# Tables, projection and the first layer's edges in one block, K and V stored ahead of Q, rings of 8 and 16 gathered chunks, and one index load for 8 chunks

## The reference, cut to what matters

```python
# layer 0, 8 heads of 16 features
Q, K, V, Eh = x @ WQ, x @ WK, x @ WV, edge_attr @ WE
score = exp(clip((K[src] * Q[dst] / sqrt(16) * Eh).sum(per head), -5, 5))
h = x + segment_sum(V[src] * score, dst) / (segment_sum(score, dst) + 1e-6)
x = layernorm(x + batchnorm(h))
# layer 1, one head
xl = x @ W
e = leaky_relu((xl @ att_src)[src] + (xl @ att_dst)[dst], 0.2)
e = exp(e - segment_max(e, dst)[dst])
out = segment_sum(e / segment_sum(e, dst)[dst] * xl[src], dst) + bias
x = layernorm(x + (bn_relu(bn_relu(out @ W1 + b1) @ W2 + b2) + x))
```

## Time and profile before

| | |
|---|---|
| Median of three runs | 5932.58 us (5929.43 to 5944.88) |
| Profiled execution | 5944.3 us, span 5942.5 us |
| PE busy, PEld busy | 4076.5 us (69%), 3506.1 us (59%) |
| DVE busy | 3282.2 us (55%) |
| ACT busy | 1399.3 us (24%) |
| POOL busy | 3368.5 us (57%), of it 3272.3 us in the 3328 gathers |
| Granted TensorE clock, mean | 0.659 |
| DMA | 482,022 packets, 538.82 MB |

### The profile page before, as it was taken

One profiled execution on the slowest core, in us unless ns is written; L12 is line 12 of the kernel. 1 busy time (PEld: TensorE's weight loads), 2 busy tenths in 40 slices (PEclk: granted clock), 3 DMA queues, 4 the chain that ended last, 5 costly groups with the idle time before them and its releaser, 6 DMA issues. The chain is left out here.

```text
span 5942.5 us, 93441 instructions
## 1 busy us (share of the span) xinstructions
PE 4076.5 (69%) x21439; PEld 3506.1 (59%) x21440; DVE 3282.2 (55%) x8432; ACT 1399.3 (24%) x4197; POOL 3368.5 (57%) x3417
## 2 busy tenths in 40 slices
PE   5888888888888888888455555555555555555553
PEld 3777787887777777777423444444444444444431
DVE  5554555555555555555474555555555555555555
ACT  2111111111111111111043222222222222222224
POOL 1565555565556555656334666666666666666621
PEclk8787877777778777878676555555555555555566
DMA  7444444444444444444522222222222222222223
GB/s 215 119 126 121 125 123 122 124 125 124 123 123 128 121 123 124 127 121 130 99 58 70 50 51 49 51 50 50 50 51 50 50 51 49 50 51 50 51 69 85
DMA packets 482022, 538.82 MB, mean 91 GB/s; under 512 B 250299, under 2 KB 341053, under 8 KB 481366
## 3 DMA queue, kind: packets, MB, share of 16 engines
q0 software_dynamic: 133120, 330.78, 21.5%
q1 hardware_dynamic: 348199, 203.99, 14.1%
q10 hardware_dynamic: 672, 3.74, 0.5%
HBM read 497.64 MB, written 40.50 MB: 91 GB/s over the span
## 5 line engine op out<-in xcount | busy, mean ns | idle before, releaser
L460 POOL DMA_INDIRECT kv_g<-kv_table,idx x1664 | 1642.8, 987 | 1242.4 <-issue 442.2
L1064 POOL DMA_INDIRECT xg<-xl_table,idx x1664 | 1629.5, 979 | 917.4 <-issue 473.2
L1092 PE MATMUL ps_sum<-pw,xg 128*128 128x64 f32 x3328 | 819.2, 428 | 523.9 <-DVE pws L1194 380.3
L1092 PEld LDWEIGHTS ps_sum<-pw,xg 128*128 128x128 f32 x3328 | 741.0, 328 | 645.9 <-DVE pws L1194 469.4
L498 PE MATMUL ps_sum<-hot,kv_g 128*128 128x64 f32 x3328 | 566.2, 325 | 267.7 <-issue 134.7
L559 DVE TENSOR_TENSOR prod<-ps_q,kv_g 128x512 f32<-128x512 f32 x416 | 286.7, 689 | 803.5 <-remote 526.8
L531 ACT ACTIVATE pex<-score 128x512 f32<-128x512 f32 x416 | 261.6, 629 | 1883.5 <-DVE score L567 1328.6
L498 PEld LDWEIGHTS ps_sum<-hot,kv_g 128*128 128x128 f32 x3328 | 502.4, 231 | 342.9 <-issue 162.2
L488 PE MATMUL ps_eh<-w,eat 128*128 128x128 f32 x3328 | 598.2, 331 | 48.5 <-issue 46.4
L491 PE MATMUL ps_q<-qw,hott 64*128 64x128 f32 x3328 | 578.1, 317 | 42.2 <-issue 40.9
L488 PEld LDWEIGHTS ps_eh<-w,eat 128*128 128x128 f32 x3328 | 548.7, 245 | 70.5 <-issue 64.7
(11 more groups left out here) (138 smaller groups left out, 5201.3 us busy)
## 6 DMA issues: line engine op xcount, KB each, us to landing
eat<-in_edges SPq DMA_DIRECT2D x416, 256.0 KB
kv_g<-kv_table,idx POOLq DMA_INDIRECT x1664
xg<-xl_table,idx POOLq DMA_INDIRECT x1664
idx<-in_src SPq DMA_DIRECT2D x832, 2.0 KB
qw<-q_table SPq DMA_DIRECT2D x416, 32.0 KB
adw<-ad_row SPq DMA_DIRECT2D x416, 32.0 KB
kv_table<-kv SPq DMA_DIRECT2D x25, 512.0 KB, 4.1
xl_table<-xl SPq DMA_DIRECT2D x25, 264.0 KB
```

Of the source, the lines that this page charges most:

```text
L460: nc.gpsimd.indirect_dma_start(out=kv[:, u, k], out_offset=None, in_=m["kv_table"], in_offset=bass.IndirectOffsetOnAxis(ap=idx[:, i, k:k + ...
L1064: nc.gpsimd.indirect_dma_start(out=xg[:, u, k], out_offset=None, in_=m["xl_table"], in_offset=bass.IndirectOffsetOnAxis(ap=idx[:, u, k:k + ...
L1092: nc.tensor.matmul(ps_sum[:, b, 0:W], xg[:, u, k, 0:D], pw[:, b, k], start=(k == 0), stop=(k == K - 1))
```

## The change

- `prologue`, `project` and `edges0` become one block. The host hands over x transposed in two orders: `xk` for the projection (loaded by ACT in 5 pieces into `acc[:, 1]`) and `xt` (loaded by SP at the start of `nodes0` in 3 pieces into a new tile `third`, which takes the part of `acc[:, 2]`). PE's transposes of x and their two copies go.
- First K and V of all groups are made and stored (ring of 3 staging tiles, ACT alone copies); then Q of all groups (ring of 2). POOL waits for the stores of K and V only, and gathers 8 chunks while Q is being made. Rows of the tables are stored 4 nodes to a partition, in pieces of 4 KB and 2 KB.
- POOL clears `acc[:, 0]` before the first gather; DVE clears `acc[:, 1]` once PE has made the last Q.
- `U, V` go from 4, 8 to 8, 16: the ring of gathered rows has 8 chunks in layer 0 and 16 in layer 1, and the loop bodies grow to 8 chunks (PE, ACT, DVE in layer 0; DVE in layer 1 as before) and 16 (SP and POOL; in layer 1 PE and ACT too). The rings of edge features, Q windows and 0/1 matrices stay at 4, that of destination terms at 8.
- Indices come in loads of 8 chunks (128 B in each of 128 partitions) into a ring of 2 such blocks. Slot p of sub-chunk k is now edge 128k + p. The last chunk, with 20 edges, is gathered by 1 indirect DMA in place of 4.
- To make room, some tiles move to PSUM: the column numbers that DVE compares with (`ps_iota`), and in layer 1 the masked logits and the fade factors. The two sums of a stage share one PSUM bank, and in layer 1 the turned and the spread maximum of a chunk do.

```diff
-U, V = 4, 8
+U, V = 8, 16
+B = 8
+STAGES = 3
...
-        prologue(nc, m, dst_rows, dst_cols, weights, vectors)
-        project(nc, m, x)
-        edges0(nc, m, src, edges)
-        far_windows0(nc, m, src, edges)
-        nodes0(nc, m)
...
+        edges0(nc, m, xk, src_cols, dst_rows, dst_cols, edges, weights, vectors)
+        far_windows0(nc, m, src_cols, edges)
+        m["third"] = sb("third", [P, NP])
+        nodes0(nc, m, xt)
...
+            for g in range(6, NG):
+                store_kv(g)
+            for u in range(4):
+                load_edges(u, u)
+            for g in range(NG):
+                sp.wait_ge(taken, 2 * NG + g + 1)
+                sp.dma_start(q_rows[g], q_out[:, g % 2].rearrange("p k d -> p (k d)")).then_inc(q_stored[g % 2], 16)
             sp.wait_ge(base_back, 48)
...
+            def body(c, v, peeled):
+                sp.wait_ge(spread, c + 1 + LEAD)
+                if not (peeled and c + 4 >= NC):
+                    load_edges(c + 4, v)
+                    load_window(c + 4, v)
+                if v % B == 5 and not (peeled and c + 11 >= NC):
+                    sp.wait_ge(kv_in[7], landed(c, v % U, 16 * K, U))
+                    load_src((c - v) * K + (v // B + 2) * (B * K), v // B)
+            over_chunks(sp, body, NC, V)
...
+            pool.wait_ge(scratch_free, 1)
+            nc.gpsimd.memset(acc[:, 0], 0.0).then_inc(clear, 1)
...
+            for s in range(STAGES):
+                pool.wait_ge(kv_stored[s], 16 * (-(-(NG - s) // STAGES)))
             for u in range(U):
                 gather(u, u)
...
+            for g in range(NG):
+                if g >= STAGES:
+                    act.wait_ge(kv_stored[g % STAGES], 16 * (g // STAGES))
+                for half in range(2):
+                    act.wait_ge(projected, 2 * g + half + 1)
+                    nc.scalar.activation(kv_out[:, g % STAGES, 2 * half:2 * half + 2].rearrange("p k d -> p (k d)"),
+                                         ps_pair[:, g % 2, half], ACT.Identity).then_inc(taken, 1)
...
             one_hot(2, 2)
+            dve.wait_ge(projected, 3 * NG)
+            nc.vector.memset(acc[:, 1], ATTN_EPS).then_inc(clear, 1)
             attend(0, 0)
...
             sp.dma_start(m["den_rows"], acc[0:P:DH, 1, :]).then_inc(den_out, 16)
+            for piece, (first, end) in enumerate(PIECES):
+                sp.dma_start(third[:, first * G:end * G], xt[:, first * G:end * G]).then_inc(xt_in[piece], 16)
             sp.wait_ge(den_out, 16)
...
             def body(c, u, peeled):
                 sp.wait_ge(largest, c + 1)
-                load_window(c + V, u)
-                sp.wait_ge(xl_in[u], landed(c, u, 16 * K, V) + past[u])
-                load_src(c + V, u)
-            over_chunks(sp, body, NC - V, V)
+                if not (peeled and c + U >= NC):
+                    load_window(c + U, u)
+                if u % B == 4 and not (peeled and c + 12 >= NC):
+                    sp.wait_ge(xl_in[u + 3], landed(c, u, 16 * K, V) + past[u + 3])
+                    load_src((c - u) * K + (u // B + 2) * (B * K), u // B)
+            over_chunks(sp, body, NC, V)
```

More of the change, by code:

```diff
@@ L165, in landed, with build @@
     return before(i, slot, each, slots) + each
-def build(nc, x, src, dst_rows, dst_cols, edges, weights, vectors, out):
+def build(nc, xt, xk, src_cols, dst_rows, dst_cols, edges, weights, vectors, out):
     with ExitStack() as ctx:
@@ L473, in _ @@
             lead(pe, [spread, summed], LEAD)
+            wkv = m["w"][:, WK:WV + 1, :].rearrange("p a d -> p (a d)")
+            pe.wait_ge(weights_in, 32)
+            for g in range(NG):
+                for piece, (first, end) in enumerate(XK_PIECES):
+                    if g == first:
+                        pe.wait_ge(xk_in[piece], 16)
+                if g >= 2:
+                    pe.wait_ge(taken, 2 * g - 2)
+                for k in range(T):
+                    mm = nc.tensor.matmul(ps_pair[:, g % 2, k // 2, at(k % 2, 2 * D)], nodes_x[:, g, k], wkv, start=True, stop=True)
+                    if k % 2 == 1:
+                        mm.then_inc(projected, 1)
+            for g in range(NG):
+                pe.wait_ge(taken, 2 * NG - 2 + g // 2 * 2 if g < 4 else 2 * NG + g - 3)
+                for k in range(T):
+                    mm = nc.tensor.matmul(ps_pair[:, 1 - g % 4 // 2, g % 2, at(k, D)], nodes_x[:, g, k], m["w"][:, WQ], start=True, stop=True)
+                mm.then_inc(projected, 1)
+            pe.wait_ge(made, 4)
+            pe.wait_ge(taken, 3 * NG)
             def turn(c, u):
@@ L517, in _ @@
         def _(act):
+            act.dma_start(m["w"][:], weights).then_inc(weights_in, 16)
+            for piece, (first, end) in enumerate(XK_PIECES):
+                act.dma_start(acc[:, 1, first * G:end * G], xk[:, first * G:end * G]).then_inc(xk_in[piece], 16)
+            act.dma_start(m["vec"][:], vectors).then_inc(weights_in, 16)
             lead(act, [copied], LEAD)
+            for g in range(NG):
+                if g >= STAGES:
[4 more added lines that the diff above has]
+                                         ps_pair[:, g % 2, half], ACT.Identity).then_inc(taken, 1)
+            for g in range(NG):
+                if g >= 2:
+                    act.wait_ge(q_stored[g % 2], 16 * (g // 2))
+                act.wait_ge(projected, 2 * NG + g + 1)
+                nc.scalar.activation(q_out[:, g % 2].rearrange("p k d -> p (k d)"), ps_pair[:, 1 - g % 4 // 2, g % 2],
+                                     ACT.Identity, scale=DH ** -0.5).then_inc(taken, 1)
             def copy_out(c, u, first=False):
@@ L1071, in body @@
                 pool.wait_ge(summed, c + 1 + LEAD)
-                gather(c + V, u)
+                gather(c + V, u, peeled and c + V == NC - 1)
             over_chunks(pool, body, NC - V, V)
```

444 lines of the change are left out of this document (181 added, 263 removed).

## The result

The changed kernel took 6037.35 us (median of four runs, 6033.40 to 6037.47) against 5931.01 us of the kernel before in the same measurement: ratio 1.0176, 95% interval 1.0155 to 1.0196. It is slower; 5920 was forecast. The profiled execution took 6033.4 us, its span is 6031.6.

A forecast was written before the change was run, and what follows sets the result against it. PE's signals, late in and behind POOL's runs of gathers, were taken to bound the edge loops. The terms -4 - 8 + 15 + 5 - 20 = -12 from 5932.6 gave 5920 us, own range 5880 to 5955.

The forecast's parts named there:

- Steady loops: Both layers' edge loops: fewer index loads, PSUM operands and larger bodies change almost nothing; -20 us, bounds -175 and +120.
- rival 2: Layer 1's loop: index blocks asked for just as POOL needs them make longer gather runs; +120 us, about 6050; chance 0.19.
- Rival 1: Edge loops: taking out 19% of the packets makes PE's signals less late; up to -175 us, about 5755; chance 0.27.
- Rival 3: Start: PE stands still through POOL's first gathers, +20 in place of -4, and +20 in layer 1; about 5960; chance 0.11.
- the start: Stretch until the first attend: first use of gathered rows at about 148 us; -4 us, bounds -40 and +20.
- Layer 1, start and end: 64 first gathers +40, 8 more chunks without gathers -20, chunks done meanwhile -15; +5 us, bounds -10 and +20.
- Rival 4: Layer 0: PE's body of 575 entries is fetched anew once a turn; 52 turns cost +114 us, 6035; chance 0.05.
- nodes0: After layer 0's edges: x's load stands ahead of the denominators' on SP's queue; +15 us, bounds 0 and +25.
- Layer 0: Layer 0's edges: the last 8 chunks in place of 4 run without a gather beside them; -8 us, bounds 0 and -10.
- the sign I denied: Loops: time per chunk moving by more than 0.05 us, either way, would show the prediction wrong.

The follow-up runs named there:

- the four variants: Changed kernel with, in layer 1, ring of 8, block asked 4 chunks sooner, per-chunk indices, or bounded outstanding gathers: 5904.2, 5930.6, 5934.3, 6019.6 us on late chips.
- the three variants of layer 0: Changed kernel with POOL only 4 chunks ahead in layer 0 (run twice), or layer 0's indices loaded per chunk: 4895.2, 4895.8 and 4867.5 us, quick chips.

## Why the prediction was wrong

**The step that failed** is "Steady loops": "Their landing is awaited by nobody before [...], so the direct gain is 0", and "Between them I take -20". Between chunks 24 and 400 layer 1 took 80 us more and layer 0 27 less. I carried what was true of the loads before (4 chunks ahead or more) to the loads after, and chose against my own working in rival 2, which had the order of SP's and POOL's steps right: the block is asked for when POOL needs it. Priced there at 2.4 us a block, 120 in all and 6050 us with a chance of 0.19, it measured: pause 4.0 us a block, all pauses together 106 us more than with the block in time, 102 us between the medians 6032.5 and 5930.6 (two chips of one kind), total 6037. My argument against it, that the pause also lets late signals through, was right for a quarter of the cost only: POOL's other pauses shrank by 0.7 us for 3 us of longer pause, and the additions come twice after some 4 us, then twice after 9 to 10. Nor did the deep ring hide the pause, as the rival itself had supposed. The ring was full of gathered rows, but everybody waits for PE's signals, and these come behind the run of gathers that makes up for the pause. That the late request costs the time is shown by the edit; this last link is read from the timeline, and no run parts the run of gathers from the pause ahead of it.

**Rival 1** (the loads count) is refuted for layer 1: per-chunk loads there changed the total by 4 us on a late chip. In layer 0 they were tried on a quick chip alone. What the Trainium skill says on merging small transfers ("DMA: Bandwidth & Descriptors", "Rules for kernel authors") had nothing to gain here: nobody waited for these loads until they were merged.

**Rival 3** (frozen start): the start came at -1.4 us against my -4, inside the bounds. In layer 1 the other half of this rival held, and the term "Layer 1, start and end" is a second one that was mis-sized: +28 us against my +5. From the first gather to the addition of chunk 24 the stage takes 236.8 us where it took 189.7, from chunk 400 on 55.2 where it took 74.5. The gathers in front cost more than the 40 us that I gave them, the 15 for chunks done meanwhile didn't come, and the 20 at the end did. It is the depth's doing: with a ring of 8 the first stretch takes 190.5 us on a late chip. With the block in time the whole stage is 2562.1 us long with a ring of 16 and 2540.9 with a ring of 8, both on one chip, and 2554.0 before the change on another. So the ring of 16 is a loss of about 20 us of its own; the totals (5930.6 and 5904.2) say 26.

**Rival 4** (fetch): the two instruction queues carried 42 packets against 31 before, fewer than one for each of the 52 turns; the loops with the large bodies run at 6.06 us per chunk once the block comes in time, so no price of it shows.

**nodes0**: +16.2 against +15, by the step as worked out (x ahead of the denominators). How much of it is the order is open: with the largest piece moved behind, the inversion started 8 us sooner on a quick chip but the stage ended only 2 to 4 us sooner, and two pieces were still ahead.

**Layer 0**: -35 us against -8 and a share of -20. Sign and place are right, the size is not. Its last 8 chunks took 4.6 us each, against a forecast of 4.7. The rest lies in the steady loop, 6.56 us per chunk in place of 6.63 (chunks 24 to 400), and in the four variants on late chips too, whose stage is 2701 to 2715. So the sign I denied, a rate that moves by more than 0.05 us, came in both layers. Ring depth and loads were tried on quick chips alone, loop bodies and PSUM operands not at all; what gives the gain on late chips stays open.

**A better version** is the ring of 8 in layer 1 with everything else kept: 0.9937 of the kernel before on a late chip, where it beats both kernels, and 0.9832 on a quick one. On quick chips it isn't shown to beat the changed kernel: layer 1's stage takes 2121.1 and 2128.2 us with it, and 2116.8 to 2121.6 in the three variants of layer 0, which leave layer 1 as it was changed. The changed kernel's 0.9881 comes from the measurement with slower gathers.

## What to carry to other kernels

When loads are merged into blocks, work out anew how far ahead of its first reader each block is asked for: the request that came 4 chunks ahead per chunk may come none ahead per block, and moving it by 4 chunks was worth 1.7% on a late chip. Don't count on a deep ring to hide a producer's pause; look at what is late behind the burst that makes up for it. And a ratio from one chip is not the ratio: time kernel and reference on several, for here the sign changed.

## What the runs showed of the hardware

The same kernel, the one before, took 5931 to 5940 us on some chips and 4960 to 4979 on others. The work is the same: in layer 1 a gather's instruction takes 0.947 us at the median in the changed kernel's first trace and 0.944 in the one from a quick chip, its rows land 1.3 and 1.2 us later, and a 4 KB packet of layer 0's gathers takes 0.16 us in both. Two things differ. PE's semaphore signals come up to 13 us late (99th percentile of the changed kernel's, 7 of the kernel before) during and behind POOL's runs of gathers on the late chips and at once on the quick ones; and SP's longer entries last 0.69 us on the late chips and 0.35 on the quick ones (90th percentile of some 8,000). What makes a chip one or the other no run here shows, nor whether it is the chip itself: the one that was used twice was quick both times.

On a late chip the granted clock of layer 0 is 0.79 and on a quick one 0.91 (the changed kernel's layer 0 and layer 1 on a quick chip, in the columns of the windows above):

```profile
131.70:2249.60 2117.90, 1999.93 (x14950) 1872.13 (x14948) 1445.37 (x2909) 459.59 (x830) 1599.34 (x1629) 0.91 0.53 159
2571.80:4692.00 2120.20, 1404.13 (x5361) 1169.58 (x5362) 1372.16 (x4534) 714.16 (x2881) 1608.46 (x1636) 0.50 0.28 59
```

PE is busy for 94% of the first stretch and for 86% on the late chip; layer 1 stays at 0.50, the lower level, on both.
